# Two stacked recurrent layers on one core: a third weight tile of layer 0 in bfloat16 parts, projections in uneven pieces, rests moved between VectorE and GpSimd

## The reference

```python
def step(h_prev, xw_t):                 # one layer
    h_next = jnp.tanh(h_prev @ Wh + xw_t)   # xw_t = x_t @ Wx + b
    return (h_next, h_next)
...
x = x + layer0(x, cond, Wx0, Wh0, b0)
x = x + layer1(x, cond, Wx1, Wh1, b1)
```

## Time and profile before

| | |
|---|---|
| median of 3 runs | 2059.51 us (2058.35 to 2059.56) |
| profiled execution, span | 2057.6 us (its own time outside the profiler is not given; the median is 1.9 us above the span) |
| PE busy | 2044.6 us, 99% of the span, 98388 MATMUL |
| PEld (weight loads) busy | 1863.8 us, 91%, 98388 LDWEIGHTS |
| DVE (VectorE) busy | 1746.3 us, 85% |
| ACT (ScalarE) busy | 1280.9 us, 62% |
| POOL (GpSimd) busy | 444.9 us, 22% |
| granted TensorE clock | 1.00 of full speed in every stretch |

### The profile page before, as it was taken

One profiled execution on the slowest core, in us unless ns is written; L12 is line 12 of the kernel. 1 busy time (PEld: TensorE's weight loads), 2 busy tenths in 40 slices (PEclk: granted clock), 3 DMA queues, 4 the chain that ended last, 5 costly groups with the idle time before them and its releaser, 6 DMA issues.

```text
span 2057.6 us, 219078 instructions
## 1 busy us (share of the span) xinstructions
PE 2044.6 (99%) x98388; PEld 1863.8 (91%) x98388; DVE 1746.3 (85%) x10221; ACT 1280.9 (62%) x6660; POOL 444.9 (22%) x2054
## 2 busy tenths in 40 slices
PE   8999999999999999999999999999999999999999
PEld 6999999999999999999999999999999999999997
DVE  5888888888888888888888888888888888888887
ACT  4666666666666666666666666666666666666665
POOL 3222222222222222222222222222222222222221
DMA  3000000000000000000000000000000000000000
GB/s 108 25 26 25 26 25 26 25 26 25 27 24 27 24 28 24 28 24 28 24 27 24 27 24 27 24 27 24 28 23 28 23 27 24 27 24 27 24 27 15
DMA packets 111960, 56.33 MB, mean 27 GB/s; under 512 B 12432, under 2 KB 111008, under 8 KB 111520
## 3 DMA queue, kind: packets, MB, share of 16 engines
q1 hardware_dynamic: 111168, 53.53, 8.8%
q10 hardware_dynamic: 576, 1.18, 0.2%
q0 software_dynamic: 32, 0.02, 0.0%
HBM read 37.90 MB, written 16.78 MB: 27 GB/s over the span
## 4 chain that ended last, share of the span: by engine, by line
PE 99%; DMA 1%; issue 0%; DVE 0%; ACT 0%; SPq 0%; ACTq 0%
PE ps_rec L270 44%; PE ps_rec L287 33%; PE ps_xw L247 22%; DMA wx<-wx_in 0%; DMA wh<-wh_in 0%; PE ps_rec L339 0%; DVE zt L463 0%; ACT h L387 0%; SPq L223 0%; ACTq L421 0%; ACTq L420 0%; DVE z L472 0%; DVE x_out L503 0%; SPq L222 0%
## 5 line engine op out<-in xcount | busy, mean ns | idle before, releaser
L270 PE MATMUL ps_rec<-wh,h 128*32 128x128 f32 x33024 | 1261.2, 273 | 3.3 <-ACT h L387 2.8
L387 ACT ACTIVATE h<-z 128x24 f32<-128x24 f32 x4066 | 654.7, 208 | 666.4 <-DVE z L472 625.0
L287 PE MATMUL ps_rec<-wh_part,h 128*32 128x128 bf16 x48792 | 1036.9, 219 | 1.5 <-issue 1.5
L270 PEld LDWEIGHTS ps_rec<-wh,h 128*32 128x32 f32 x33024 | 880.0, 109 | 30.1 <-ACT h L387 6.7
L287 PEld LDWEIGHTS ps_rec<-wh_part,h 128*32 128x32 bf16 x48792 | 724.0, 96 | 151.1 <-issue 1.8
L205 POOL TENSOR_TENSOR h<-h 128x16 f32<-128x16 f32 x2032 | 430.6, 212 | 1589.9 <-DVE h L205 1589.9
L472 DVE TENSOR_REDUCE z<-zt 128x24 f32<-128x72 f32 x4066 | 664.5, 205 | 69.7 <-DVE zt L463 0.6
L376 ACT ACTIVATE ps_rec<-ps_xw,mask 128x128 f32<-128x128 f32 x2048 | 664.2, 324 | 77.9 <-PE ps_xw L247 77.9
L463 DVE STREAM_TRANSPOSE zt<-ps_rec 128x128 f32<-128x128 f32 (+1 forms) x2063 | 649.8, 316 | 18.7 <-PE ps_rec L270 12.7
L205 DVE TENSOR_TENSOR h<-h 128x16 f32<-128x16 f32 x2034 | 356.0, 175 | 209.2 <-ACT h L387 0.2
L247 PE MATMUL ps_xw<-wx,x_pe 128*32 128x128 f32 x8248 | 404.6, 273 | 2.0 <-issue 1.1
(11 more groups left out here) (20 smaller groups left out, 16.5 us busy)
## 6 DMA issues: line engine op xcount, KB each, us to landing
x_pe<-x_t SPq DMA_DIRECT2D x256, 64.0 KB, 2.0
x_dve<-x_t SPq DMA_DIRECT2D x256, 64.0 KB, 1.9
out_t<-x_out SPq DMA_DIRECT2D x256, 64.0 KB, 1.5
wh<-wh_in SPq DMA_DIRECT2D x1, 1024.0 KB, 5.7
wx<-wx_in SPq DMA_DIRECT2D x1, 1024.0 KB, 8.3
wx<-wx_in ACTq DMA_DIRECT2D x1, 512.0 KB, 5.2
wx<-wx_in SPq DMA_DIRECT2D x1, 512.0 KB, 5.0
wh<-wh_in SPq DMA_DIRECT2D x1, 512.0 KB, 7.2
```

Of the source, the lines that this page charges most:

```text
L270: mm = pe.matmul(rows(ps_rec[l][n % 2], g), h_step(l, n - 1)[:, k, :], wh[l][:, k, g * P:(g + 1) * P], start=False, stop=k == KC - 1 and n ...
L287: mm = pe.matmul(rows(ps_rec[l][n % 2], g), h_bits(l, n - 1)[:, k, :], wh_part[l][:, i, at:at + P], start=False, stop=k == KB[l] - 1 and i ...
L387: act.activation(h_of(l, n)[:, tiles, :], src[:, tiles, :], ACT.Tanh).then_inc(h_count(l, n)[0], 1)
```

## The change

1. `KB = (3, 2)`: layer 0 takes three tiles in parts and one whole. Its third tile's weights are made into parts by GpSimd at the start.
2. Projections come in pieces. A slot has one half tile and one full tile in its first place and one half tile in its second; a half tile is the left or the right 64 of the 128 columns.
3. VectorE transposes and sums in two halves of two tiles each (it was one transpose of four tiles, and sums of three tiles and one), and tanh follows in the same halves.
4. Rests: for layer 0, VectorE makes both rests of tiles 0 and 1 (`rests`), and GpSimd both of tile 2. For layer 1, GpSimd makes both.
5. TensorE waits for the rests of layer 0 twice (tiles 0 and 1, then tile 2), and `recur_whole` waits for the second piece of tanh only. The loop stays at eight slots.

```diff
-KB = (2, 2)
+KB = (3, 2)
-PROJECT = (((0, 3), (1, 0)), ((1, 1), (1, 2)), ((1, 3), (0, 0)), ((0, 1), (0, 2)))
+BOTH, LEFT, RIGHT = slice(0, P), slice(0, P // 2), slice(P // 2, P)
+PROJECT = ((0, ((2, RIGHT), (3, BOTH)), 1, ((0, LEFT),)), (1, ((0, RIGHT), (1, BOTH)), 1, ((2, LEFT),)),
+           (1, ((2, RIGHT), (3, BOTH)), 0, ((0, LEFT),)), (0, ((0, RIGHT), (1, BOTH)), 0, ((2, LEFT),)))
...
-            def project(l, c, k):
+            def project(l, c, k, cols=BOTH):
...
-                    mm = pe.matmul(rows(ps_xw[l][c % 2], g), src, wx[l][:, k, g * P:(g + 1) * P], start=False,
-                                   stop=False, skip_group_check=True, tile_position=(0, 32 * g))
+                    mm = pe.matmul(rows(ps_xw[l][c % 2], g)[:, cols], src, wx[l][:, k, g * P:(g + 1) * P][:, cols],
+                                   start=False, stop=False, skip_group_check=True, tile_position=(0, 32 * g))
...
-                    elif k == pieces(l, n - 1)[1].start:
-                        pe.wait_ge(*h_count(l, n - 1))
+                    elif k % 2 == 0 or k == in_parts(l, n):
+                        pe.wait_ge(*h_count(l, n - 1, k // 2))
...
-                pe.wait_ge(*split_count(l, n - 1))
                 for k in range(KB[l]):
+                    if k % 2 == 0:
+                        pe.wait_ge(*split_count(l, n - 1, k // 2))
...
             for l, n in ORDER:
                 if is_split(l, n):
-                    pool.wait_ge(rest_done[l], n + 1 if l else n + 2 - PARTED)
-                    rest(pool, l, n, 2).then_inc(split_count(l, n)[0], S4 if (l, n) == (0, PARTED - 1) else 1)
+                    mine, done = (rest_done[1], n + 1) if l else (late_done, n + 2 - PARTED)
+                    tiles = HALVES[0] if l else slice(2, 3)
+                    if l and (n + LAG) % S4 == S4 - 1 and n + LAG < T:
+                        pool.wait_ge(mid_done, (n + LAG) // S4 + 1)
+                    pool.wait_ge(*h_count(l, n, 1 - l))
+                    rest(pool, l, n, 1, tiles).then_inc(mine, 1)
+                    pool.wait_ge(mine, done)
+                    rest(pool, l, n, 2, tiles).then_inc(split_count(l, n, 1 - l)[0], S4 if (l, n) == (0, PARTED - 1) else 1)
...
-                for tiles in HALVES if is_whole(l, n) else (slice(0, KC),):
+                for tiles in HALVES:
...
-            def rest_first(l, n):
-                if is_split(l, n):
-                    dve.wait_ge(*h_count(l, n, 0))
-                    rest(dve, l, n, 1).then_inc(rest_done[l], 1)
+            def rests(n):
+                if is_split(0, n):
+                    dve.wait_ge(*h_count(0, n, 0))
+                    rest(dve, 0, n, 1).then_inc(rest_done[0], 1)
+                    dve.wait_ge(rest_done[0], n + 2 - PARTED)
+                    rest(dve, 0, n, 2).then_inc(split_count(0, n, 0)[0], S4 if n == PARTED - 1 else 1)
```

More of the change, by code:

```diff
@@ L34 @@
 LAYERS = (0, 1)
-PIECES = (slice(0, KC - 1), slice(KC - 1, KC))
 HALVES = (slice(0, KC // 2), slice(KC // 2, KC))
@@ L118, in build @@
         rest_done = [sem(f"rest{l}_done") for l in LAYERS]
-        split_done = [[sem(f"split{l}_done{j}") for j in range(2)] for l in LAYERS]
+        late_done = sem("late_rest0_done")
+        split_done = [[[sem(f"split{l}_{i}_done{j}") for j in range(2)] for i in range(2 - l)] for l in LAYERS]
         mid_done = sem("mid_done")
@@ L148, in is_split, with zt_count, split_count @@
             return n < T - 1 and not is_whole(l, n + 1)
[L150 to L157, removed]
+        def zt_count(n, piece):
+            return 2 * n + piece + 1
         def z_count(l, n, piece):
             return 2 * (n if l else n - PARTED) + piece + 1
-        def split_count(l, n):
+        def split_count(l, n, i=0):
             s = n + LAG * l
-            return split_done[l][s // S4 % 2], s % S4 + 1
+            return split_done[l][i][s // S4 % 2], s % S4 + 1
         block = ctx.enter_context(nc.Block())
@@ L200, in x_of, with rest @@
             return xs[n // S4 % 2][:, :].rearrange("p (k s b) -> p s k b", s=S4, b=B)[:, n % S4]
-        def rest(eng, l, n, part):
-            step, to, of, tiles = h_step(l, n), h_cols(n, part), h_cols(n, part - 1), slice(0, KB[l])
+        def rest(eng, l, n, part, tiles=HALVES[0]):
+            step, to, of = h_step(l, n), h_cols(n, part), h_cols(n, part - 1)
             return eng.tensor_tensor(step[:, tiles, to], step[:, tiles, of], h_bits(l, n)[:, tiles, of], ALU.subtract)
@@ L293, in projection @@
             def projection(s, half):
-                l, k = PROJECT[s % S4][half]
+                l, pieces = PROJECT[s % S4][2 * half:2 * half + 2]
                 c = (s - S4) // S4 if l else (s + 6) // S4
                 if 0 <= c < NG or l == 0 and s < T:
-                    if k == 0 and l == 0:
+                    if pieces[0] == (0, LEFT) and l == 0:
                         pe.wait_ge(seed0_done[c % 2], 1)
-                    if k == 0 and (l, c) == (1, 0):
+                    if pieces[0] == (0, LEFT) and (l, c) == (1, 0):
                         pe.wait_ge(s_wx1, DMA)
-                    if k == 0 and l == 1 and c in (0, NG - 1):
+                    if pieces[0] == (0, LEFT) and l == 1 and c in (0, NG - 1):
                         pe.wait_ge(mid_done, c + 1)
-                    project(l, c, k)
+                    for k, cols in pieces:
+                        project(l, c, k, cols)
             def slot(s):
@@ L315, in slot @@
                     pe.wait_ge(x_first[1], DMA)
-                    for k in range(KC - 1):
-                        project(0, 1, k)
+                    for k, cols in ((0, BOTH), (1, BOTH), (2, LEFT)):
+                        project(0, 1, k, cols)
                 projection(s, 0)
@@ L379, in tanh @@
             def tanh(l, n):
-                for i, tiles in enumerate(pieces(l, n)):
+                for i, tiles in enumerate(HALVES):
                     if is_whole(l, n):
-                        act.wait_ge(zt_done[l], zt_count(l, n, i))
+                        act.wait_ge(zt_done[l], zt_count(n, i))
                         src = rows_of_h(l, n)
@@ L469, in total @@
                 at = LOWEST[n % S4] * B
-                dve.wait_ge(zt_done[l], zt_count(l, n))
-                for tiles in PIECES:
+                for i, tiles in enumerate(HALVES):
+                    dve.wait_ge(zt_done[l], zt_count(n, i))
                     dve.tensor_reduce(z[l][n % 2][:, :].rearrange("p (k b) -> p k b", k=KC)[:, tiles, :],
@@ L517, in slot @@
                 if n0 is not None:
-                    rest_first(0, n0)
+                    rests(n0)
                 if n1 is not None:
```

33 lines of the change are left out of this document (15 added, 18 removed).

## The result

| | before | after |
|---|---|---|
| median | 2059.28 us of 4 runs (2058.35 to 2059.56) | 3990.6 us of 4 runs (3989.96 to 3996.43) |
| ratio, 95% interval | | 1.9387 (1.9359 to 1.9414) |
| span of the profiled execution | 2057.6 us | 3988.1 us |
| granted TensorE clock over the span | 1.00 | 0.883 |

The account below looks back on a forecast made before the run. It took TensorE's matmuls as the bound, at 1.98 us a slot, with the data loop as long. 2060 to 2070 us plus 445 for one refetched block a pass gave 2505 us, range 2030 to 3950.

Parts of the forecast that it names:

- The code's length: TensorE's loop body grows to eight blocks plus a ninth fetched ahead; one block refetched each pass, 445 us; chance 0.33.
- rival A: TensorE's loop code: every block comes again in each pass, 3750 to 4600 us, 3920 at 3.6 a fetch; chance 0.25.
- up to 4.7: Jump back of TensorE's loop: highest price in us a pass, if the fetch ahead has to finish first.
- whenever the last one is entered: TensorE's loop end: the ninth block, at pair 1501, is fetched ahead each time the body's last block is entered.
- The price of one code stall at the jump: TensorE's jump back to a block not held: 2.9 to 3.5 us a pass, up to 4.7, taken as 3.5.
- The third tile on TensorE: Layer 0's third tile in parts: minus 0.22 plus 0.165, -0.055 us a slot; a half projection tile 0.11.
- TensorE's own need of 1.925: TensorE's matmul time in us a slot after the change; if it ruled, 56 us would go, giving 2004 us.
- The loop over the data: Layer 0's step from parts through transpose, sum, tanh and rests to the next parts: 1.99 us, bounds 1.90 to 2.13.
- Rival D: Code stays held and the first half sum starts 0.26 to 0.33 after the transpose: faster, 2020 us at 0.30; chance 0.15.
- Rival B: More than eight blocks fit and the data loop rules: 1.985 to 2.13 a slot, 2064 to 2212 us; chance 0.21.
- Layer 1 and GpSimd: Layer 1's step with both rests on GpSimd takes 1.99 us; GpSimd's four instructions of 0.21 a slot don't queue long.

Follow-up runs that it names:

- pad40: The changed kernel with ten more rounds of four warm-up matmuls ahead of the loop (WARM 10 to 20), body from pair 640: 2394.5 us, one run.
- pad8: The changed kernel with two more rounds of four warm-up matmuls (WARM 10 to 12), body from pair 608: 2084.4 us, 1.013 times before.
- pad4: The changed kernel with one more round of four warm-up matmuls (WARM 10 to 11), body from pair 604: 3999.8 us, one run.
- defer_begin: pad8 with ScalarE's copy of a projection that seeds layer 1's bank moved behind layer 0's tanh: 2069.0 us, 1.0048 times before.
- l1_on_vector: pad8 with layer 1's first rest on VectorE as before the change, the second on GpSimd: 2089.1 us, 1.0141; one more run of 4757.6 us.

## Why the prediction was wrong

**The step that failed** is the one under "The code's length" that says the ninth block "displaces one in each of 127 passes, and the one displaced must come again at the jump back". I priced that at 445 us and took it as likelier than rival A, "every block comes again", against which I held that one lost block "is the least that must happen". All of them come again: nine packets a pass, pad40's 21 passes at nine each. That is as if the ninth block turned out the one that will be needed first, and that one, coming back, the next. Had the ninth shared a fixed place with one block alone, two packets a pass would have come. The prediction had worked the first of these out as A, at 29 to 36 us a pass and 3920 us. A pass is 30.2 and 31.8 us in the windows, 31.0 from the difference to pad8 ((3988.1 - 2082.3) / 127 = 15.0, on 16.0), and the kernel 3990.6. So the case that came true was in the text with its size right within 2%, at a chance of 0.25, and the range was cut at 3950, inside it. The sentence that stands behind it held too: the Trainium skill, "Runtime: NRT & Kernel Launch", section "Instruction fetch mechanics", speaks of a FIFO, and by that rule it had to be this case. The trace agrees that all blocks come again. Whether they leave in order of age or a jump to a missing block empties the store isn't told apart by these runs, since both give nine fetches a pass. The working had two slips that decide nothing: the terms of "up to 4.7" add up to 4.8, and A's seven fetches of 4.0, 1.7 and one more give 33.7 us a pass and not 36.

**What held on the code.** The body touching eight blocks from five pairs ahead of the boundary at 605: pad4 and pad8 lie on its two sides, 3999.8 and 2084.4 us. Eight as the number held: pad40's quiet passes hold eight, and with the ninth nothing stays. The Trainium skill, "Advanced Engine Details and Errata", section "ISA Cache", states 128 KB in lines of 256 instructions, and the trace agrees with both figures (18.79 MB in 1147 packets are 16.4 KB each, and eight of them are held). A fetch of 3.4 to 4.0 us: the stalls stand 3.5 to 4.0 apart. That the fetch ahead is made "whenever the last one is entered" was too strong: with three pairs left before the jump it was made in 21 passes of 126.

**The price of one code stall at the jump** (2.9 to 3.5, up to 4.7) was not far off: TensorE stood idle for 3.65 us there, and the first matmul behind it came 3.98 us after the branch (1020.91 - 1016.93).

**The third tile on TensorE.** 36 matmuls in parts take 0.51 from start to start (1000.20 to 1000.71; I said 0.50), and the projection of three half tiles' columns 0.33 (1000.71 to 1001.04), 0.11 each. TensorE's own need of 1.925 can't be read off, since the data rule; an estimate is 1.94, the mean slot of 2.00 less the 65.5 us that the weight loads of the parts waited for VectorE, 0.06 a slot.

**The loop over the data.** Forecast 1.99 for layer 0's step, measured 1.97. To the transposes 0.73 against 0.74; to the first sum 0.35 against 0.30; the rest 0.91 against 0.93. Rival D, faster, was to decide itself on a sum at 0.30, and there it lies; but D wanted 1.94 from it and got 1.97, because the transposes come 0.01 and the parts behind the rests 0.02 later than I had. The mean slot was 2.00, from two things that no term had: the copy on ScalarE ahead of tanh (0.015 a slot, defer_begin) and the longer slot that the jump stands in (0.08 in eight slots, 0.01 a slot; its cause is open). Rival B, "likeliest 2070": with the code held pad8 takes 2084.4, within B's range. The change is slower than before even then.

**Layer 1 and GpSimd** as forecast: at four rests a slot the parts hardly wait for GpSimd (1.0 us in pad8's run), and l1_on_vector shows no difference. At five they do.

No kernel here beats that of before; the best, defer_begin, is 10 us behind it.

## What to carry to other kernels

Count the instructions of a hardware loop's body against the blocks of code that the engine holds, with where it starts and with the block fetched ahead behind it: here seven blocks cost nothing, eight and the ninth ahead nearly doubled the time, and eight pairs of padding took off 1906 us of the 1931. One block too many meant that all were missed, so the least that must happen is not always what happens. When a chain over data is as long as the engine's work, an edit that frees the engine and lengthens the chain loses (0.055, an estimate, against 0.17 here), and the other engines' copies ahead of the chain's instructions are then worth moving first (15 us for two lines).

## What the runs showed of the hardware

- TensorE held eight blocks of 128 pairs. A ninth, fetched ahead and not run in the loop, made each of the eight come again in every pass, at 3.5 to 4.0 us a block, for 2.4 us of work (16.0 us a pass, times 128 / 864).
- After a jump to a block that was held, the first weight load came 0.26 us after the branch; to one that wasn't, 4.0 us after (1020.91), and 3.6 to 4.3 over the run.
- The block behind was mostly not fetched when the jump followed three pairs after its predecessor was entered (105 passes of 126).
- The granted clock fell to 0.50 within a stretch of 7.2 us in which TensorE ran only 0.35 us of matmuls, and stayed there for an estimated 6.8 us (from 0.61, 0.50 and 0.96 over three windows). It stood at 1.00 between stalls of about 1 us.
- On VectorE an increment by two put the transpose's wait into an instruction of its own, 0.07 us more from the parts to the transpose (0.81 against 0.74).
